# Query and key rows laid out by pair of batches in 28-row blocks, and the score products that feed the maximum made twice

## What is computed

```python
x = x + diffuse(x)                    # zX*lap_x + zY*lap_y + zR*x*(1-x), per batch
x = x + experts(x)                    # 8 experts and a shared one, D=128, F=512:
                                      # sum of gate * (silu(x@Wg) * (x@Wu)) @ Wd
x = x + lora(x, language)             # two products by rank 16 and an embedding
x = x + attention(x, side)            # 16 heads of 8 features
# queries, and for each query one more key and value (its own token's), come from `side`;
# the 128 other keys and values from x. q = (side + b_self)@Wq + bq, k = (x + b_prev)@Wk + bk
# score_prev = q.k / sqrt(8), masked beyond seq_len; score_self = (q*k_self).sum
# weights = softmax(concat(score_prev, score_self)); out = weights @ values @ Wo + bo
```

## Time and profile before

| | |
|---|---|
| three runs | 499.92, 500.70, 501.67 us, median 500.70 |
| the profiled execution, its own time | 500.33 us |
| its span, first to last instruction | 497.1 us |
| mean granted clock of TensorE | 0.943 of 2.4 GHz |
| busy, share of the span | TensorE 91%, VectorE 69%, ScalarE 54%, GpSimd 39% |
| moved by DMA | 37.31 MB in 44730 packets |
| stages | experts to about 379 us (first tile to about 109 us), attention to 497.1 us |

### The profile page before, as it was taken

One profiled execution on the slowest core, in us unless ns is written; L12 is line 12 of the kernel. 1 busy time (PEld: TensorE's weight loads), 2 busy tenths in 40 slices (PEclk: granted clock), 3 DMA queues, 4 the chain that ended last, 5 costly groups with the idle time before them and its releaser, 6 DMA issues.

```text
span 497.1 us, 7804 instructions
## 1 busy us (share of the span) xinstructions
PE 450.9 (91%) x2278; PEld 328.2 (66%) x2278; DVE 344.3 (69%) x634; ACT 267.4 (54%) x544; POOL 191.7 (39%) x187
## 2 busy tenths in 40 slices
PE   6889899789999999999999999999997879978795
PEld 2667678567787887777788776887884434434442
DVE  5398567586777789677778967776875655766562
ACT  2457657465464664546466454646555434545463
POOL 4456676882132533113253311333773121222220
PEclk9689989899999999999999999999999785989889
DMA  5324333220004011000401000032107266455620
GB/s 152 112 79 112 122 86 112 79 67 1 2 7 125 3 63 42 0 0 6 123 2 62 21 1 0 7 104 65 61 22 195 64 176 180 141 168 167 179 74 22
DMA packets 44730, 37.31 MB, mean 75 GB/s; under 512 B 4216, under 2 KB 39196, under 8 KB 44700
## 3 DMA queue, kind: packets, MB, share of 16 engines
q1 hardware_dynamic: 43248, 36.64, 25.4%
q0 software_dynamic: 1024, 0.26, 0.3%
q10 hardware_dynamic: 432, 0.10, 0.1%
HBM read 26.07 MB, written 10.66 MB: 74 GB/s over the span
## 4 chain that ended last, share of the span: by engine, by line
PE 59%; DVE 11%; DMA 8%; SPq 8%; issue 5%; ACT 5%; POOL 3%; ACTq 0%; DVEq 0%
PE acc_ps L550 6%; SPq L460 5%; PE g_ps L550 5%; PE g_ps L552 5%; PE g_ps L551 5%; PE acc_ps L552 5%; PE acc_ps L551 5%; DVE act_lo L1103 4%; DMA w_raw<-in_L_cond_Wu 4%; PE u_ps L550 4%; PE u_ps L552 4%; PE u_ps L551 4%; DVE act_p L1099 3%; PE st_ps L718 3%; PE pv_ps L730 3%
## 5 line engine op out<-in xcount | busy, mean ns | idle before, releaser
L837 ACT ACTIVATE act_p<-g_ps 128x512 f32<-128x512 f32 x144 | 86.1, 598 | 135.4 <-PE g_ps L552 120.2
L1099 DVE TENSOR_TENSOR act_p<-act_p,u_ps 128x512 f32<-128x512 f32 x144 | 98.5, 684 | 72.9 <-PE u_ps L552 45.3
L1103 DVE TENSOR_TENSOR act_lo<-act_p,act_hi 128x512 fp32r<-128x512 f32 x144 | 121.9, 846 | 0.2 <-ACT act_hi L842 0.2
L1305 POOL TENSOR_TENSOR xg_lo<-xg,xg_hi 128x512 fp32r<-128x512 f32 x35 | 50.2, 1433 | 149.4 <-ACT xg_hi L847 149.4
L842 ACT ACTIVATE act_hi<-act_p 128x512 fp32r<-128x512 f32 x144 | 89.8, 624 | 4.8 <-DVE act_p L1099 4.7
L550 PE MATMUL acc_ps<-act_hi,w_split 128*128 128x512 f32 x144 | 62.1, 431 | 15.7 <-DVE act_lo L1103 15.6
L933 ACT ACTIVATE probs_t<-st_ps 128x512 f32<-128x512 f32 x64 | 38.2, 597 | 47.6 <-PE st_ps L718 47.5
L550 PE MATMUL g_ps<-x_hi,w_split 128*128 128x512 f32 (+1 forms) x144 | 58.6, 407 | 1.4 <-DVE x_lo L1128 1.4
L551 PE MATMUL g_ps<-x_lo,w_split 128*128 128x512 f32 (+1 forms) x144 | 57.7, 400 | 0.0
L552 PE MATMUL g_ps<-x_hi,w_split 128*128 128x512 f32 (+1 forms) x144 | 57.6, 400 | 0.0
L550 PE MATMUL u_ps<-xg_hi,w_split 128*128 128x512 f32 x144 | 57.1, 397 | 0.0
(11 more groups left out here) (147 smaller groups left out, 715.9 us busy)
## 6 DMA issues: line engine op xcount, KB each, us to landing
k_blocks<-k_rows SPq DMA_DIRECT2D x32, 96.0 KB
q_plain<-q_rows SPq DMA_DIRECT2D x8, 384.0 KB
q_blocks<-q_rows SPq DMA_DIRECT2D x32, 96.0 KB
k_plain<-k_rows SPq DMA_DIRECT2D x8, 384.0 KB
v_both<-v_d SPq DMA_DIRECT2D x8, 272.0 KB, 3.6
w_raw<-in_L_cond_Wg SPq DMA_DIRECT2D x8, 256.0 KB, 2.9
w_raw<-in_L_cond_Wu SPq DMA_DIRECT2D x8, 256.0 KB, 3.1
w_raw<-in_L_cond_Wd SPq DMA_DIRECT2D x8, 256.0 KB, 2.9
```

Source lines behind the costliest of these rows:

```text
L837: activation(act_p[k % 3][:], g_ps[k % 3][:], ACT.Silu).then_inc(silu_done, 1)
L1099: tt(act_p[k % 3][:], act_p[k % 3][:], u_ps[k % 3][:], ALU.mult).then_inc(prod_done, 1)
L1103: tt(act_lo[k % 3][:], act_p[k % 3][:], act_hi[k % 3][:].bitcast(F32), ALU.subtract).then_inc(act_lo_done, 1)
L1305: tt(xg_lo[e % 3][:], xg[:].rearrange("p b s -> p (b s)"), xg_hi[e % 3][:].bitcast(F32), ALU.subtract)\
```

## The change

The rows are laid out in DRAM by pair: q_rows and k_rows are (8 pairs, 112 rows, 4, 256). A block j has 28 rows: its 24 as before, one row of ones (queries) or the mask (keys), and three of zeros. The mask thus lies in each block, and the row of ones with it; the separate mask loads (L466, L477) and the copies of ones (L519) go. A row of a pair is one piece of 1024 numbers in DRAM and in SBUF, where it was four of 256. For this k_blocks and q_blocks are ordered (j, i) and no longer (i, j). Each store of a tile is made in two halves, one for each pair. The pads come from a constant input and are written once behind the first tile, by two DMAs; the mask is written by four where it was one. The contraction is over 112 rows (97 before) and over 114 (99 before).

Apart from this, each score product for the maximum is issued twice into the same bank (SCORE_RUNS), with the same operands and start=True, except the eight early ones inside the last tile's experts; VectorE is released by the second.

```diff
 GI, GJ = 4, 4
-ROW_MASK = 3 * DH * GJ
-ROW_MAX = ROW_MASK + 1
+BLOCK_MASK = 3 * DH
+BLOCK_ROWS = BLOCK_MASK + 4
+ROW_MAX = BLOCK_ROWS * GJ
 Q_SLOTS, K_SLOTS = ((0, 2), 1), ((0, 1), 2)
...
 NP = B // PAIR
+ROW_STORES = 16 * 3 * TB // PAIR
...
 AHEAD = 3
+SCORE_RUNS = 2
...
-        q_rows = dram("q_rows", (ROW_MASK, GI, B * S))
-        k_rows = dram("k_rows", (ROW_MASK + 1, GI, B * S))
+        q_rows = dram("q_rows", (NP, ROW_MAX, GI, PAIR * S))
+        k_rows = dram("k_rows", (NP, ROW_MAX, GI, PAIR * S))
         mask_row = dram("mask_row", (B, S))
...
             for n in range(2):
-                blocks.append(sb2(f"{names[0]}{n}", [128, GI, GJ, PAIR * S], F32R))
+                blocks.append(sb2(f"{names[0]}{n}", [128, GJ, GI, PAIR * S], F32R))
                 plain.append(sb2(f"{names[1]}{n}", [128, GI, PAIR * S], F32R))
...
-            def store_rows(dst, tok, places):
-
-                of_place = dst[0:ROW_MASK].rearrange("(j s r) i n -> j s (r i) n", j=GJ, s=3)
+            def store_rows(dst, t, places):
+
                 his, lo = places
-                for s in his:
-                    sp.dma_start(of_place[:, s, :, tok], rows_hi[:].bitcast(F32)).then_inc(rows_stored, 16)
-                sp.dma_start(of_place[:, lo, :, tok], rows_lo[:].bitcast(F32)).then_inc(rows_stored, 16)
+                for rows, s in [(rows_hi, s) for s in his] + [(rows_lo, lo)]:
+                    for m in range(TB // PAIR):
+                        to = dst[t * (TB // PAIR) + m].rearrange("(j x) i n -> j x i n", j=GJ)[:, s * DH:(s + 1) * DH]
+                        sp.dma_start(to.rearrange("j r i n -> j (r i) n"),
+                                     rows[:, m * PAIR * S:(m + 1) * PAIR * S].bitcast(F32)).then_inc(rows_stored, 16)
...
                     sp.dma_start(mask_row, mask_sb[:]).then_inc(mask_stored, 16)
+            for rows, first in ((q_rows, 0), (k_rows, 1)):
+                to = rows.rearrange("p (j x) i n -> p j x (i n)", j=GJ)[:, :, BLOCK_MASK + first:BLOCK_ROWS]
+                sp.dma_start(to.rearrange("p j x n -> p j (x n)"),
+                             a["row_pads"][first:].rearrange("x n -> (x n)").unsqueeze(0).unsqueeze(0)
+                             .to_broadcast([NP, GJ, (BLOCK_ROWS - BLOCK_MASK - first) * GI * PAIR * S])).then_inc(pads_stored, 16)
             sp.wait_ge(mask_stored, 16)
-            sp.dma_start(k_rows[ROW_MASK:], mask_row.rearrange("b s -> (b s)").unsqueeze(0).unsqueeze(0)
-                         .to_broadcast([1, GI, B * S])).then_inc(later_stored, 16)
+            for j in range(GJ):
+                sp.dma_start(k_rows[:, BLOCK_ROWS * j + BLOCK_MASK],
+                             mask_row.rearrange("(p b) s -> p (b s)", b=PAIR).unsqueeze(1).to_broadcast([NP, GI, PAIR * S]))\
+                    .then_inc(later_stored if j == 0 else mask_stored, 16)
             with sp.Fori(1, NT - 1) as t:
...
-            def load_blocks(dst, src, tok, semaphore):
+            def load_blocks(dst, src, p, semaphore):
...
                 for j in range(GJ):
-                    r = slice(3 * DH * j, 3 * DH * (j + 1))
-                    sp.dma_start(dst[r, :, j].bitcast(F32), src[r, :, tok]).then_inc(semaphore, 16)
+                    r = slice(BLOCK_ROWS * j, BLOCK_ROWS * (j + 1))
+                    sp.dma_start(dst[r, j].bitcast(F32).rearrange("r i n -> r (i n)"),
+                                 src[p, r].rearrange("r i n -> r (i n)")).then_inc(semaphore, 16)
+
+            def load_plain(dst, src, p, semaphore):
+                sp.dma_start(dst[0:ROW_MAX].bitcast(F32).rearrange("r i n -> r (i n)"),
+                             src[p].rearrange("r i n -> r (i n)")).then_inc(semaphore, 16)
...
-                tok = bass.ds(p * PAIR * S, PAIR * S)
-                load_blocks(k_blocks[m % 2], k_rows, tok, first_loaded[m % 2])
-                sp.dma_start(k_blocks[m % 2][ROW_MASK:ROW_MASK + 1].rearrange("p i j n -> p (i j) n").bitcast(F32),
-                             mask_row.rearrange("b s -> (b s)").unsqueeze(0).unsqueeze(0)[:, :, tok]
-                             .to_broadcast([1, H, PAIR * S])).then_inc(first_loaded[m % 2], 16)
-                sp.dma_start(q_plain[m % 2][0:ROW_MASK].bitcast(F32), q_rows[:, :, tok]).then_inc(first_loaded[m % 2], 16)
+                load_blocks(k_blocks[m % 2], k_rows, p, first_loaded[m % 2])
+                load_plain(q_plain[m % 2], q_rows, p, first_loaded[m % 2])
...
-                tok = bass.ds(p * PAIR * S, PAIR * S)
-                load_blocks(q_blocks[m % 2], q_rows, tok, second_loaded[m % 2])
-                sp.dma_start(k_plain[m % 2][0:ROW_MASK].bitcast(F32), k_rows[0:ROW_MASK, :, tok])\
-                    .then_inc(second_loaded[m % 2], 16)
-                sp.dma_start(k_plain[m % 2][ROW_MASK:ROW_MASK + 1].bitcast(F32), k_rows[ROW_MASK:ROW_MASK + 1, :, tok])\
-                    .then_inc(second_loaded[m % 2], 16)
+                load_blocks(q_blocks[m % 2], q_rows, p, second_loaded[m % 2])
+                load_plain(k_plain[m % 2], k_rows, p, second_loaded[m % 2])
...
-            sp.wait_ge(rows_stored, 16 * 3 * (2 * NT - 1))
+            sp.wait_ge(rows_stored, ROW_STORES * (2 * NT - 1))
             sp.wait_ge(later_stored, 16 * (1 + 2 * (NT - 1)))
+            sp.wait_ge(mask_stored, 16 * GJ)
+            sp.wait_ge(pads_stored, 32)
             for m in range(2):
...
                 sp.wait_ge(blocks_filled, 2 * (m + 3))
-
-                sp.dma_start(q_blocks[m][ROW_MASK:ROW_MASK + 1].rearrange("p i j n -> p (i j) n").bitcast(F32),
-                             k_plain[m][127:128, 0:1].bitcast(F32).to_broadcast([1, H, PAIR * S])).then_inc(ones_placed, 16)
                 load_second(m, m)
...
                 if i == 0:
-                    pe.wait_ge(first_loaded[n // 2 % 2], loaded(b, n, 6))
+                    pe.wait_ge(first_loaded[n // 2 % 2], loaded(b, n, 5))
                 wait(pe, max_done, b * GI + i - (1 if bank is None else 0))
-                mm((s_ps[i % 2] if bank is None else bank)[:], q_plain[n // 2 % 2][0:ROW_MASK + 1, i, half(n)],
-                   k_blocks[n // 2 % 2][0:ROW_MASK + 1, i, :, half(n)], start=True, stop=True).then_inc(s_written, 1)
+                for _ in range(1 if bank is not None else SCORE_RUNS):
+                    last = mm((s_ps[i % 2] if bank is None else bank)[:], q_plain[n // 2 % 2][0:ROW_MAX, i, half(n)],
+                              k_blocks[n // 2 % 2][0:ROW_MAX, :, i, half(n)], start=True, stop=True)
+                last.then_inc(s_written, 1)
...
                 mm(st_ps[i % 2][:], k_plain[n // 2 % 2][0:ROW_MAX + 2, i, half(n)],
-                   q_blocks[n // 2 % 2][0:ROW_MAX + 2, i, :, half(n)], start=True, stop=True).then_inc(st_written, 1)
+                   q_blocks[n // 2 % 2][0:ROW_MAX + 2, :, i, half(n)], start=True, stop=True).then_inc(st_written, 1)
...
                 own = self_score[:, b].rearrange("p (i j) -> p i j", i=GI)
-                part = neg_max[n % 2][:].rearrange("p c (i j) -> p c i j", i=GI)
+                part = neg_max[n % 2][:].rearrange("p c (j i) -> p c i j", i=GI)
                 dve.wait_ge(max_done, b * GI + GI)
...
                     pool.dma_start(q_blocks[n // 2 % 2][ROW_MAX + c:ROW_MAX + c + 1, :, :, n % 2 * S:(n % 2 + 1) * S]
-                                   .rearrange("p i j s -> p (i j) s").bitcast(F32),
+                                   .rearrange("p j i s -> p (j i) s").bitcast(F32),
                                    max_rows[n % 2][c * H:(c + 1) * H]).then_inc(max_placed[n % 2], 16)
```

More of the change, by code:

```diff
@@ L246, in build @@
         mask_stored = sem("mask_stored")
+        pads_stored = sem("pads_stored")
         dif_step, z_step, gate_step, small_cast = sem("dif_step"), sem("z_step"), sem("gate_step"), sem("small_cast")
@@ L263, in build @@
         cols_spread = sem("cols_spread")
-        blocks_filled, ones_placed = sem("blocks_filled"), sem("ones_placed")
+        blocks_filled = sem("blocks_filled")
         first_loaded = [sem(f"first_loaded{n}") for n in range(2)]
@@ L393, in later_stores @@
                 sp.wait_ge(aux_drained, n + 3)
-                store_rows(k_rows, bass.ds(t * N, N), K_SLOTS)
+                store_rows(k_rows, t, K_SLOTS)
                 sp.wait_ge(aux_drained, n + 4)
@@ L405, in first_store @@
                     sp.wait_ge(aux_drained, aux_of(kind, f) + 1)
-                    store_rows(q_rows, bass.ds(f * N, N), Q_SLOTS)
+                    store_rows(q_rows, f, Q_SLOTS)
                 if kind == "natural" and b == TB - 1:
@@ L530, in _ @@
             step(-1, 1, out=False, x3=False)
-            sp.wait_ge(rows_stored, 16 * 3 * 2 * NT)
+            sp.wait_ge(rows_stored, ROW_STORES * 2 * NT)
             sp.wait_ge(later_stored, 16 * (1 + 2 * NT))
@@ L714, in scores_t @@
                 if i == 0:
-                    pe.wait_ge(second_loaded[n // 2 % 2], loaded(b, n, 6))
+                    pe.wait_ge(second_loaded[n // 2 % 2], loaded(b, n, 5))
```

(6 more changed lines are left out.)

## The result

| | median of all executions, us | span of the profiled one | first value load to the end | batches 4 to 14 |
|---|---|---|---|---|
| before | 501.19 (499.92 to 519.98, 4) | 497.1 | 117.4 | 64.9 |
| changed | 511.31 (506.29 to 512.57, 4) | 509.4 | 133.6 | 78.5 |

One of the four executions of the kernel before, 519.98 us, fell in a slower state of the chip, and each ratio of this document leaves such executions out on both sides. The changed kernel is slower: the ratio is 1.019, with a 95% interval of 1.010 to 1.028. The forecast was 499.0 us, between 493 and 505. The profiled execution took 511.44 us.

A forecast was written before the change was run, and what follows sets the result against it. The prediction took SyncE's load-issue queue to pace the attention loop, not the bytes. From 500.33 us, -5.9 (loop) + 2.8 (opening) + 2.4 (stores) gave 499.6; with a little issue saving it forecast 499.0 us, range 493 to 505.

The forecast's parts named there:

- the queue's round: SyncE's load issues per pair in the attention loop: 13.3 to 11.8 us, so -5.9 us from batch 4 to 14.
- My bound from below: Block loads on SyncE's queue might issue like the plain load's 0.61 us: 2.7 us less, a round of 9.1.
- rival 1: Everything clears: block issues fall toward 0.61 us, clock stays up, stores lose nothing; 493 to 496 us, chance 0.16.
- rival 3: Stores dominate: 2.4 us per set in the first tile, again before batches 3 and 4; 502 to 504 us, chance 0.12.
- The prediction's own sign of being wrong: Attention loop: full-clock batch over 6 us, or 2 us waits with clock drops, or up-weight waits growing over 2 us each.
- The doubled products: Attention loop: two of four extra products per batch absorbed in waits; full-clock batch 5.20 to 5.65 us, pair 11.3.
- The waits that I expected the doubled products to fill: TensorE's waits of 0.26 us before the result's transpose and some 0.2 before two transposes, each taking one doubled product.
- Rival 2: Doubled products at full price, nothing absorbed: 56 x 0.23 = 12.9 us; 504 to 508 us, chance 0.12.
- The opening: Start of the attention loop, batches 0 to 3: doubled products +5.3 us, less gains at entry and in waits; +2.8 us.
- The stores: First tile: half-size stores with 1 KB runs delay the up weights by 1.2 us for each of two sets, +2.4 us.
- my bound from the loads: Stores of 1 KB runs at the loads' 19 GB/s per busy engine: 10.2 us a set instead of 7.9.
- rival 4: The queue is still the pace: 28-row issues dearer by a tenth, round 12.5 us; 502, or 500 with free stores, chance 0.13.

The follow-up runs named there:

- experiment 5: Changed kernel with two unused numbers behind each 256 in the SBUF row buffers, so loads have runs of 1 KB: 493.28 us, ratio 0.982 to before.
- experiment 3: Changed kernel with the second half of a pair's loads held until the odd batch's maxima are placed: 495.30 us, ratio 0.986 to before.
- experiment 4: Changed kernel without the transfers that place the maxima, exponentials on scores scaled by 0.1, no maximum subtracted: 490.52 us, ratio 0.977 to before.
- experiment 9: Changed kernel, runs of 4 KB kept, with a tiny transfer behind each block load to space the issues: 497.36 us, ratio 0.985 to before.
- experiment 2: Kernel before with only the doubled score products added: 500.66 us, no ratio given.
- experiment 1: Changed kernel with each score product made once, so the layout alone: 509.28 us, ratio 1.014 to before.

## Why the prediction was wrong

**The step that failed is the queue's round.** I wrote that the eight block loads "stay" and took them "as they are", 0.95 us each with the gap, for a round of 11.8 us. They take 0.40 to 0.52 in the loop, and experiment 5 shows why: 28 rows with four runs each take 0.90 to 1.03, so the four rows more cost next to nothing and the runs within a row nearly everything. My bound from below, the 0.61 of the plain load, was not low enough, since that load also had four runs a row; in one run it takes 0.32. It was also set without its gap against 0.95 with the gap. A faster issue was in the range as a gain only (rival 1, 493 to 496).

**What stood in its place is a mechanism that I had not priced.** SyncE's slow issue had spread the loads evenly over the 13 us. Without it, they come in one burst as soon as TensorE lets the buffers go, and that is the moment at which GpSimd places the maxima of the odd batch. The prediction has no term for how long this placement takes when they do. The two 8 KB transfers then take up to 7.5 us in the loop, TensorE stands 1.5 to 3.8 us before batches 3, 7 and 11, and pays a second time with the half clock behind it. I saw the wait of 2.1 us for these rows, but used it in rival 3 alone, as an effect of the opening, at 1.5 us. The prediction's own sign of being wrong, waits of 2 us in the loop and a clock that drops with them, came true. Experiments 3, 4, 5 and 9 take away the coincidence in four ways, and each is 14 to 21 us below the changed kernel in the median, 3.3% to 4.2% by the ratios (2.4% for 9 against the fastest executions of the kernel before on its chip).

**The doubled products** were sized nearly right. I forecast 5.65 us for a batch at full clock that waits for no load; the changed kernel has 5.70 (batch 12, 482.36 to 488.06) and experiment 4 has 5.71. The pair was given as 11.3 and is 11.4. One thing I had missed makes them cheaper than I thought: batch 5 of the kernel before, with single products, already took 5.70 us (424.03 to 429.73), and batches 6 and 10 took 5.20 and 5.22. So at full clock this one pair, 5 and 6, pays 0.5 us for its eight extra products, not 0.9. With loads that wait, they cost 3.4 to 5.7 us over batches 4 to 14 (experiments 2 and 1, one profile each). The waits that I expected the doubled products to fill did shrink: for VectorE's normalisation TensorE waits 4 times, 2.3 us, after, and 11 times, 4.3 us, before. Rival 2, the full price, is excluded.

**The opening** was given as +2.8 us, from +3.3 inside batches 0 to 4 and -0.5 at the entry. It measured +1.8 and -3.1. The entry is not the change's to that extent: over all kernels with the new layout the first load of values is issued between 374.3 and 378.8 us, without it at 377.8 and 379.7.

**The stores** were given 1.2 us a set, +2.4, and cost nothing. ScalarE's two waits for the up weights in the first tile are, after:

```profile
55.55 0.63 ACT L817 ACTIVATE w_split<-w_raw 128x512 fp32r<-128x512 f32 x1 [1.86 <-DMA w_raw<-in_L_cond_Wu]
...
87.53 0.63 ACT L817 ACTIVATE w_split<-w_raw 128x512 fp32r<-128x512 f32 x1 [2.76 <-DMA w_raw<-in_L_cond_Wu]
```

They were 1.97 and 3.41 us. The stores alone, from 174 to 178 us, run at 93 GB/s with a share of 0.27:

```profile
174.00:178.00 4.00, 4.00 (x20) 3.36 (x19) 3.00 (x6) 2.05 (x4) 0.88 (x2) 1.00 0.27 93
```

Per busy engine that is 21.5 GB/s against 24 of before; by these rates the 768 KB of a set take 8.5 us instead of 7.9 (an estimate), and my bound from the loads (19) was too slow. By the Trainium skill ("DMA: Bandwidth & Descriptors", Specifications) 1 KB is past the least transfer for line rate and would lose nothing. The trace has a tenth less, so it agrees with that rule only nearly; that the kernel loses nothing is seen in the two waits above.

**The sum.** With the measured terms it is 500.33 - 3.1 (all up to the entry) + 1.8 (batches 0 to 4) + 13.6 (4 to 14) + 0.1 - 1.2 (around the span, 2.0 us where it was 3.2) = 511.5, against 511.44 measured. Batches 4 to 14 alone miss the forecast by 19.5 us (+13.6 instead of -5.9); the other terms, -2.4 together where I had +4.6, give 7.0 of it back. That the time missed the upper end of the range by 6 us only is luck of these other terms. Two more points of the working: rival 4 adds up to 503.1 and 500.7 with its own terms, not 502 and 500, and the 0.3% by which a measurement was to be told from no change is far less than the spread of 506.3 to 512.6 us that the changed kernel has.

**What stays open.** Where in the DMA engines the small transfers wait is not shown: the trace gives their issue and landing, not the engine that holds them. Nor is it shown why batch 5 takes longer than batch 6 with single products; of the 0.5 us, 0.28 is a wait for VectorE's maximum at 428.71, of which batch 6 has none. It is open as well why a load of 28 rows in four runs takes longer to issue (0.82 us without its gap in experiment 5) than one of 112 rows in four runs (0.62).

## What to carry to other kernels

A slow issuing engine can be what spreads the traffic. Before making its issues cheaper, look for the small transfer that a waiting engine needs and that is issued at the moment at which the large loads are released, and ask how long it takes when they all come at once. If it is on the path, hold or space the loads around it, by one means and not by two: here a wait for the small transfer's semaphore or a dearer issue won 14 to 18 us of median over the burst, and both together only 7.

## What the runs showed of the hardware

- What SyncE pays for a transfer goes mostly by the runs within a row, hardly by bytes: with its gap, a load of 28 rows in one run of 4 KB each takes 0.40 to 0.52 us in the loop, of 28 rows in four runs of 1 KB each 0.90 to 1.03, of 24 rows in four runs 0.96. Without it, 112 rows in one run take 0.32, 112 rows in four runs 0.62, 96 rows in four runs 0.61.
- Loads issued at this pace bring the DMA share to 0.92 in a 4 us window at 226 GB/s. Two transfers of 8 KB that land in 1.7 us at the end of the kernel then take 6.4 to 7.5. Over the whole attention the longest is 7.8 us on GpSimd's queue and 8.0 on ScalarE's.
- At a share of 0.68 to 0.72 from 424 to 448 us, with 171 to 199 GB/s (experiments 5 and 9), the same small transfers land within 4.4 and 2.8 us in the loop. It takes the even pace, not less traffic: experiment 9 loads the same 1792 KB a pair as the changed kernel, and moves 199 GB/s in that window, where the changed kernel, which stands in part of it, moves 122.
- Work that TensorE repeats can cost too little to be seen. With each score product made twice, two kernels were no slower than with it made once, within some 3 us.
